# Layer-norm's beta added to three output tiles by an accumulating SBUF-to-SBUF transfer that GpSimd issues, in place of three GpSimd additions

## The chip, the cores and the metric

One core of one Trainium2 chip. The metric is the device time of one execution in microseconds (us). Engines go by the profile's names: PE is TensorE (PEld its weight loads), DVE is VectorE, ACT is ScalarE, POOL is GpSimd, SP is SyncE, which here only issues transfers.

## The reference

Cross-attention of 16 batches of 512 rows with a context of 120 rows each, a residual, and a layer norm:

```python
B, T, E, M, L = 16, 512, 512, 120, 256
q = emb @ Wq + bq                     # (B, T, E)
k = latent @ Wk + bk                  # (B, M, E)
v = latent @ Wv + bv
w = softmax(q @ k.T / sqrt(E), axis=1)      # over the 512 rows
x = w @ v + emb
mu, var = mean(x, -1), var(x, -1)
out = (x - mu) * rsqrt(var + 1e-6) * gamma + beta
```

Everything is float32, and gamma and beta are drawn, not ones and zeros.

## The kernel before

One batch is 128 partitions by four tiles j = 0 to 3 of 512 elements (`RJ` = 4). The program is software-pipelined in slots: in slot s, PE turns x of batch s and computes its scores, and multiplies probabilities and values of batch s-1; DVE adds the residual of batch s-1 and takes part of its statistics; ACT, POOL and DVE apply the norm to batch s-2. Slots 2 to 13 come from a loop over four slots, the others (0, 1, 14 to 17) are written out. Every engine has its own program, in the order of the code, and they meet at semaphores.

The norm of a batch, one slot after its statistics:

- ACT, `normalise` (lines 619 to 625): for tiles 0 to 2 (`POOL_J` = 3) it writes x*rstd + shift into `obuf[:, k % 2]`, one of two output buffers of four tiles each. It waits for POOL's `shift` and for `obuf_free`, the landing of the store that emptied this buffer.
- POOL, `times_gamma` (line 963) and `plus_beta` (line 970): three multiplications by gamma and three additions of beta, in place.
- DVE, `center` (line 825) and `rescale` (line 832): the same for tile 3 in two instructions. `center` stands in the middle of the softmax of batch s-1: after its `softmax_bias` (795 to 800) and ahead of `softmax_scale` (805, 807), for whose result ACT's `probs_to_high` (611), DVE's `probs_to_low` (811) and PE's `product` (426) wait. It, too, waits for `obuf_free` (line 824).
- POOL then finishes the statistics of batch s-1: mean of squares (982), var + eps (986, 989), `rstd` (996), `shift` (1001). DVE's part of them ends with line 899. ACT's `normalise` of the next slot waits for `shift`.
- SP (lines 307 to 326) in slot s: the context of batch s+2 (289), x of batch s+1 (285) once that ring place is free, then the store of batch s-3 (325), which waits for `pool_out` and `dve_out`. SP waits in order: what is behind a store waits with it.

So POOL's slot is: `v_part` low half (956), gamma three times, beta three times, statistics, `rstd`, `shift`. The buffer that slot s fills is used again in slot s+2. In slots 16 and 17 POOL has one tile and DVE three; slot 17 uses the buffer of slot 15, whose store is the last one that SP issues whole.

The lines that set the store and its buffer's next use:

```python
sp.wait_ge(pool_out, POOL_J * (s - 2) - moved(s - 1))          # 323
sp.wait_ge(dve_out, s - 2)
sp.dma_start(out[...], obuf[:, (k + 1) % 2]).then_inc(obuf_free[(k + 1) % 2], 16)
act.wait_ge(obuf_free[k % 2], obuf_fills(k, r))                # 622, and DVE at 824
```

Of the kernel before, what the change touches and what calls it, by code (L numbers as in the profile page):

```python
# [37 lines left out]
P = 128  # L38
# [27 lines left out]
def cross_attention(nc, x, ctx_in, Wq, bq, Wk, bk, Wv, bv, gamma, beta, out):  # L66
# [11 lines left out]
    with ExitStack() as stack:  # L78
# [19 lines left out]
        bk_all = sb("bk_all", [P, E])  # L98
        bv_all = sb("bv_all", [P, E])
        gamma_all = sb("gamma_all", [P, E])  # L100
        beta_all = sb("beta_all", [P, E])
        junk = sb("junk", [P, EC + LC + 1, E])
        act_junk = sb("act_junk", [P, B * L + LC * E], F16)
        act_warm = sb("act_warm", [P, RJ])
# [125 lines left out]
        shift_done = sem("shift_done")  # L230
        norm_done = sem("norm_done")
        pool_gamma = sem("pool_gamma")
        pool_out = sem("pool_out")
        dve_gamma = sem("dve_gamma")
        dve_out = sem("dve_out")
        tail_out = [[sem(f"tail_out{b}_{j}") for j in range(RJ)] for b in range(TAIL)]
# [45 lines left out]
        @block.sync  # L282
        def _(sp):
            def load_x(b, k):
                sp.dma_start(xbuf[:, k], x[bass.ds(b, 1)].rearrange("o (p j) e -> p (o j) e", j=RJ))\
                    .then_inc(x_in[k], 16)

            def load_ctx(b, k):
                sp.dma_start(ctx_nat[:, k, 0:L], ctx_in[bass.ds(b, 1)].rearrange("o m l -> m (o l)"))\
                    .then_inc(ctx_loaded[k], 16)  # L290

            sp.dma_start(wk_nat[:], Wk.rearrange("(c p) f -> p c f", p=P)).then_inc(wk_in, 16)
            for h in range(2):
                f = slice(h * E // 2, (h + 1) * E // 2)
                sp.dma_start(wq_nat[:, :, f], Wq.rearrange("(c p) f -> p c f", p=P)[:, :, f]).then_inc(wq_in[h], 16)
            load_ctx(0, 0)
            all_v = ctx_all.rearrange("m (b l) -> m b l", l=L)
            for h in range(2):
                sp.dma_start(all_v[:, h * B // 2:(h + 1) * B // 2],
                             ctx_in[h * B // 2:(h + 1) * B // 2].rearrange("b m l -> m b l"))\  # L300
                    .then_inc(ctx_all_in[h], 16)
            load_x(0, 0)
            sp.dma_start(wv[:], Wv.rearrange("(c p) e -> p c e", p=P)).then_inc(wv_in, 16)
            load_ctx(1, 1)
            sp.dma_start(bv_all[:], bv.partition_broadcast(P)).then_inc(bv_in, 16)

            def slot(s, k, r):

                if is_in(s, 2, B - 2):
                    sp.wait_ge(ctx_turned, s - 1)  # L310
                    sp.wait_ge(key_done, s - 1)
                if is_in(s, 0, B - 2):
                    load_ctx(s + 2, (k + 2) % RING)
                if is_in(s, 3, B - 1):
                    sp.wait_ge(norm_done, POOL_J * (s - 2))
                    sp.wait_ge(dve_gamma, (RJ - POOL_J) * (s - 2))
                if is_in(s, 0, B - 1):
                    load_x(s + 1, (k + 1) % RING)
                if is_slot(s, 0):
                    sp.dma_start(gamma_all[:], gamma.partition_broadcast(P)).then_inc(norm_in, 16)  # L320
                    sp.dma_start(beta_all[:], beta.partition_broadcast(P)).then_inc(norm_in, 16)
                if is_in(s, 3, B + 3 - TAIL):
                    sp.wait_ge(pool_out, POOL_J * (s - 2) - moved(s - 1))
                    sp.wait_ge(dve_out, s - 2)
                    sp.dma_start(out[bass.ds(s - 3, 1)].rearrange("o (p j) e -> p (o j) e", j=RJ),
                                 obuf[:, (k + 1) % 2]).then_inc(obuf_free[(k + 1) % 2], 16)

            slots(sp, slot, loop_from=3, end=B + 3 - TAIL)

            for b in range(B - TAIL, B):  # L330
                share = pool_share(b + 2)
                for j in (*range(share, RJ), *range(share)):
                    sp.wait_ge(tail_out[b - B + TAIL][j], 1)
                    sp.dma_start(out[b].rearrange("(p j) e -> p j e", j=RJ)[:, j], obuf[:, b % 2, j])\
                        .then_inc(tail_stored, 16)
            for q in range(2):
                sp.wait_ge(obuf_free[q], 16 * ((B - TAIL) // 2 + 1))
            sp.wait_ge(tail_stored, 16 * TAIL * RJ)
# [332 lines left out]
        def _(dve):  # L671
# [115 lines left out]
            def slot(s, k, r):  # L787
# [40 lines left out]
                def rescale(j):  # L828

                    dve.wait_ge(rstd_done, s - 1)  # L830
                    dve.wait_ge(dve_gamma, (RJ - POOL_J) * (s - 2) + moved(s) + j - groups[0] + 1)
                    done = dve.scalar_tensor_tensor(obuf[:, k % 2, j, :], obuf[:, k % 2, j, :],  # L832
                                                    rstd[:, k % 2, j:j + 1], beta_all[:], ALU.mult, ALU.add)
                    if is_slot(s, B) or is_slot(s, B + 1):
                        done.then_inc(tail_out[s - B][j], 1)
                    elif j == RJ - 1:
                        done.then_inc(dve_out, 1)
# [29 lines left out]
                if is_slot(s, 1):  # L867
                    ctx_to_low(2, 2)
                    copy_v(1, 1)
                    dve.wait_ge(norm_in, 2 * 16)  # L870
                if is_in(s, 2, B - 1):
                    copy_v(s + 1, k + 1)
                if is_in(s, 1, B):
# [57 lines left out]
        def _(pool):  # L931
# [14 lines left out]
            for q in range(2):  # L946
                pool.sem_inc(obuf_free[q], 16)
            pool.wait_ge(constants_set, 3)
            pool.wait_ge(norm_in, 2 * 16)

            def slot(s, k, r):
                share = pool_share(s)
                if is_in(s, 0, B):

                    pool.wait_ge(v_high, s + 1)
                    pool.tensor_tensor(v_part[:, k % 2, LOW], v_scaled[:, k % 2], v_part[:, k % 2, HIGH],  # L956
                                       ALU.subtract).then_inc(v_low, 1)

                def times_gamma():

                    for j in range(share):
                        pool.wait_ge(norm_done, POOL_J * (s - 2) - moved(s) + j + 1)
                        pool.tensor_tensor(obuf[:, k % 2, j, :], obuf[:, k % 2, j, :], gamma_all[:], ALU.mult)\  # L963
                            .then_inc(pool_gamma, 1)

                def plus_beta():

                    for j in range(share):
                        pool.wait_ge(pool_gamma, POOL_J * (s - 2) - moved(s) + j + 1)
                        done = pool.tensor_tensor(obuf[:, k % 2, j, :], obuf[:, k % 2, j, :], beta_all[:], ALU.add)  # L970
                        done.then_inc(pool_out if is_in(s, 2, B) else tail_out[s - B][0], 1)

                if is_in(s, 2, B + 2):
                    times_gamma()
                if is_in(s, 2, B) or is_slot(s, B + 1):
                    plus_beta()
                if is_in(s, 1, B + 1):

                    squares = SQUARE_J if is_in(s, 1, B - 1) else RJ
                    pool.wait_ge(squares_done,  # L980
                                 SQUARE_J * s if squares < RJ else SQUARE_J * (B - 2) + RJ * (s - B + 2))
                    pool.tensor_tensor(square_mean[:, 0:squares], square_sum[:, 0:squares],  # L982
                                       one_over_e[:, 0:squares], ALU.mult).then_inc(square_mean_done, 1)
                    if squares < RJ:
                        pool.wait_ge(aggr_done, (RJ - SQUARE_J) * s)
                        pool.tensor_tensor(var_eps[:, squares:], mean_var[:, squares:, 1], eps_all[:, squares:],  # L986
                                           ALU.add)
                    pool.wait_ge(square_mean_done, s)
                    pool.tensor_tensor(var_eps[:, 0:squares], square_mean[:, 0:squares], eps_all[:, 0:squares],  # L989
                                       ALU.add).then_inc(var_ready, 1)  # L990
                    if is_slot(s, B):
                        pool.wait_ge(dve_out, s - 2)
                    elif is_in(s, 2, B):
                        pool.wait_ge(dve_out, s - 1)
                    pool.wait_ge(var_ready, s)
                    pool.tensor_tensor(rstd[:, (k + 1) % 2], var_eps[:], minus_half[:], ALU.pow)\  # L996
                        .then_inc(rstd_done, 1)
                    if squares < RJ:
                        pool.wait_ge(mean_negated, s)
                    pool.wait_ge(rstd_done, s)  # L1000
                    pool.tensor_tensor(shift[:], neg_mean[:, (k + 1) % 2, 0:POOL_J], rstd[:, (k + 1) % 2, 0:POOL_J],  # L1001
                                       ALU.mult).then_inc(shift_done, 1)
                if is_slot(s, B):
                    plus_beta()

# [23 lines left out]
```

## Time and profile before

| | |
|---|---|
| median of 3 runs | 229.74 us (229.37 to 231.14) |
| the profiled execution | 232.62 us, span 230.8 us |
| busy share of the span | PE 86%, DVE 81%, POOL 75%, ACT 70% |
| granted TensorE clock, mean | 0.941 of full speed |
| instructions of POOL | 192 |

The span runs from the first to the last instruction; what the profiled execution has beyond it lies outside. Times in rows are from the span's start. A timeline row gives start, duration, engine, line, operation, output and inputs, shapes and count; in brackets stands the idle time ahead of it and what ended it. Neighbouring rows overlap a little, since an instruction is read in while the one before it is written.

### The profile page before, as it was taken

The numbers are of one execution on the slowest core, as the hardware profiler recorded it, in microseconds if no ns is written. First come the engines' busy times: TensorE is split into PE (matmuls) and PEld (weight loads), VectorE is DVE, ScalarE is ACT, GpSimd is POOL, SyncE is SP. The second block draws the span as 40 slices with busy tenths as digits, with TensorE's granted clock in tenths as the row PEclk, the third lists the DMA queues.
The fourth block names the chain that finished last, engine by engine and source line by source line (L and its number), as shares of the span: only waits on it lengthen the run. The fifth ranks groups of instructions, "written<-read, shape, count | busy, mean of one in ns | idle before, by whom it ended". The sixth has DMA issues, their size and how long they took to land.

```text
span 230.8 us, 4222 instructions
## 1 busy us (share of the span) xinstructions
PE 197.4 (86%) x1168; PEld 120.6 (52%) x1168; DVE 187.6 (81%) x452; ACT 161.5 (70%) x343; POOL 173.4 (75%) x192
## 2 busy tenths in 40 slices
PE   4699599999999998999799989898999898999000
PEld 4546467657566565656455555555555555545000
DVE  0472845688989898979999898999898989869993
ACT  2426465589887888787887878787969696877610
POOL 1000100428999999999999999999999999999792
PEclk9769769999999999999999999999999999999855
DMA  6999976001364737364545555555455454040454
GB/s 152 295 209 293 351 263 227 0 4 23 159 217 172 227 162 226 159 216 170 203 182 203 182 203 182 203 182 203 182 203 182 182 183 182 3 182 1 182 191 173
DMA packets 11914, 41.04 MB, mean 178 GB/s; under 512 B 1022, under 2 KB 5886, under 8 KB 8062
## 3 DMA queue, kind: packets, MB, share of 16 engines
q1 hardware_dynamic: 11614, 40.37, 50.4%
q10 hardware_dynamic: 288, 0.52, 1.3%
q8 instruction: 5, 0.08, 0.2%
q14 instruction: 7, 0.06, 0.1%
HBM read 24.12 MB, written 16.78 MB: 177 GB/s over the span
## 4 chain that ended last, share of the span: by engine, by line
POOL 56%; issue 16%; DMA 9%; PE 7%; DVE 5%; DVEq 1%; ACT 1%; SPq 1%; POOLq 1%
POOL obuf L963 20%; POOL obuf L970 18%; DMA obuf<-in_ctx 8%; POOL rstd L996 6%; POOL v_part L956 6%; POOL square_mean L982 3%; PE g_ps L404 2%; PE s_ps L434 2%; DMA out<-obuf 2%; POOL var_eps L986 1%; POOL var_eps L989 1%; DVE obuf L832 1%; DVEq L78 1%; PE v_ps L393 1%; PE xT_ps L412 1%
## 5 line engine op out<-in xcount | busy, mean ns | idle before, releaser
L963 POOL TENSOR_TENSOR obuf<-obuf,gamma_all 128x512 f32<-128x512 f32 x44 | 61.0, 1411 | 1.6 <-ACT obuf L624 1.6
L970 POOL TENSOR_TENSOR obuf<-obuf,beta_all 128x512 f32<-128x512 f32 x44 | 57.9, 1344 | 0.1
L434 PE MATMUL s_ps<-xT,gT 128*120 128x512 f32 x120 | 54.7, 598 | 0.0
L426 PE MATMUL pv_ps<-v_part,prob_part 120*128 120x512 f16 x135 | 36.1, 381 | 7.6 <-DVE xbuf L843 3.0
L624 ACT ACTIVATE obuf<-xbuf,shift,rstd 128x512 f32<-128x512 f32 x44 | 32.8, 805 | 11.3 <-POOL shift L1001 11.3
L561 ACT ACTIVATE xT<-xT_ps 128x512 f32<-128x512 f32 x64 | 34.3, 588 | 5.1 <-PE xT_ps L412 5.1
L412 PEld LDWEIGHTS xT_ps<-ident,xbuf 128*128 128x128 f32 x256 | 30.4, 143 | 11.4 <-issue 8.6
L434 PEld LDWEIGHTS s_ps<-xT,gT 128*120 128x120 f32 x120 | 22.2, 186 | 24.8 <-issue 16.2
L412 PE MATMUL xT_ps<-ident,xbuf 128*128 128x128 f32 x256 | 34.2, 278 | 1.1 <-DMA xbuf<-in_x 0.9
L843 DVE SCALAR_TENSOR_TENSOR xbuf<-pv_ps,back_y,xbuf 128x512 f32<-128x512 f32 x45 | 32.4, 741 | 0.1
L956 POOL TENSOR_TENSOR v_part<-v_scaled,v_part 120x512 f16<-120x512 f32 x16 | 19.6, 1222 | 14.8 <-ACT v_part L594 14.3
L567 ACT ACTIVATE gT<-g_ps,u_col,back_g 128x120 f32<-128x120 f32 x64 | 23.6, 457 | 6.2 <-PE g_ps L404 6.2
L832 DVE SCALAR_TENSOR_TENSOR obuf<-obuf,rstd,beta_all 128x512 f32<-128x512 f32 x20 | 27.5, 1392 | 0.0
L615 ACT ACTIVATE square_junk<-xbuf,neg_mean 128x512 f32<-128x512 f32 x36 | 25.7, 716 | 0.9 <-POOL square_mean L982 0.6
L404 PE MATMUL g_ps<-ctxT,qk_part 128*128 128x120 f16 x384 | 23.9, 222 | 1.9 <-DVE qk_part L738 1.8
L404 PEld LDWEIGHTS g_ps<-ctxT,qk_part 128*128 128x128 f16 x384 | 22.5, 101 | 3.1 <-ACT qk_part L573 2.0
L426 PEld LDWEIGHTS pv_ps<-v_part,prob_part 120*128 120x128 f16 x135 | 10.4, 97 | 24.9 <-DVE prob_part L811 7.1
L393 PE MATMUL v_ps<-wv_part,ctxT 128*120 128x512 f16 x96 | 23.4, 379 | 0.0
L856 DVE BATCH_NORM_STATS2 stats<-xbuf 128x6 f32<-128x512 f32 x28 | 19.3, 689 | 0.5
L996 POOL TENSOR_TENSOR rstd<-var_eps,minus_half 128x4 f32<-128x4 f32 x16 | 16.6, 1040 | 2.2
L605 ACT ACTIVATE s_ps<-s_ps,s_bias 120x512 f32<-120x512 f32 x15 | 9.9, 663 | 11.5 <-DVE s_bias L800 11.4
L742 DVE SCALAR_TENSOR_TENSOR ctxT<-ctx_ps,scale,ctxT 128x240 f16<-128x240 f32 x16 | 7.5, 468 | 11.3 <-ACT ctxT L557 11.3
(122 smaller groups left out, 278.0 us busy)
## 6 DMA issues: line engine op xcount, KB each, us to landing
xbuf<-in_x SPq DMA_DIRECT2D x16, 1024.0 KB, 4.8
out<-obuf SPq DMA_DIRECT2D x14, 1024.0 KB, 4.2
out<-obuf SPq DMA_DIRECT2D x8, 256.0 KB, 2.5
ctx_nat<-in_ctx SPq DMA_DIRECT2D x16, 120.0 KB, 4.3
obuf<-in_ctx SPq DMA_DIRECT2D x2, 960.0 KB, 15.5
wq_nat<-in_L_xattn_Wq SPq DMA_DIRECT2D x2, 512.0 KB, 8.9
wk_nat<-in_L_xattn_Wk SPq DMA_DIRECT2D x1, 512.0 KB, 5.8
wv<-in_L_xattn_Wv SPq DMA_DIRECT2D x1, 512.0 KB, 13.9
```

What stands on the lines that cost most here:

```text
L404: mm = pe.matmul(g_v[:, e, :], qk_part[:, of_w, c, e * P:(e + 1) * P], ctxT[:, k % 2, of_ctx, c, :], start=(n == 0), stop=(n == len(steps) ...
L412: mm = pe.transpose(xT_ps[e % 2][:, j, :], xbuf[:, k, j, e * P:(e + 1) * P], ident[:])
L426: mm = pe.matmul(banks[j], prob_part[:, of_p, j * P:(j + 1) * P], v_part[:, k % 2, of_v, :], start=(n == 0), stop=(n == len(PASSES) - 1))
L434: mm = pe.matmul(s_bank(s)[0:M, :], gT[:, k % 2, e, :], xT[:, e, :], start=(e == 0), stop=(e == EC - 1))
L561: act.activation(xT[:, e, :].rearrange("p (j q) -> p j q", q=P), xT_ps[e % 2][:], ACT.Copy)\
L624: act.activation(obuf[:, k % 2, j, :], xbuf[:, kn, j, :], ACT.Identity, bias=shift[:, j:j + 1], scale=rstd[:, k % 2, j:j + 1]).then_inc(no ...
L832: done = dve.scalar_tensor_tensor(obuf[:, k % 2, j, :], obuf[:, k % 2, j, :], rstd[:, k % 2, j:j + 1], beta_all[:], ALU.mult, ALU.add)
L843: dve.scalar_tensor_tensor(xbuf[:, kb, j, :], (last_y_ps if is_slot(s, B) else y_ps)[j], back_y[:], xbuf[:, kb, j, :], ALU.mult, ALU.add, ...
L956: pool.tensor_tensor(v_part[:, k % 2, LOW], v_scaled[:, k % 2], v_part[:, k % 2, HIGH], ALU.subtract).then_inc(v_low, 1)
L963: pool.tensor_tensor(obuf[:, k % 2, j, :], obuf[:, k % 2, j, :], gamma_all[:], ALU.mult)\
L970: done = pool.tensor_tensor(obuf[:, k % 2, j, :], obuf[:, k % 2, j, :], beta_all[:], ALU.add)
L996: pool.tensor_tensor(rstd[:, (k + 1) % 2], var_eps[:], minus_half[:], ALU.pow)\
```

## The change

`beta_all` becomes three copies of beta side by side (three loads in place of one), so that one transfer can cover tiles 0 to 2. In slots 2 to 15 POOL no longer adds beta; at the end of its slot, behind `shift`, it issues one transfer with `accum_op=add` from `beta_all` to `obuf[:, k % 2, 0:3]` (128 partitions by 1536 float32, 768 KB). SP's store waits for that transfer's semaphore (`beta_added`, one for each buffer) in place of `pool_out`. Slots 16 and 17 keep their one addition on POOL.

```diff
-        beta_all = sb("beta_all", [P, E])
+        beta_all = sb("beta_all", [P, POOL_J, E])
...
-        pool_out = sem("pool_out")
+        beta_added = [sem(f"beta_added{q}") for q in range(2)]
...
-                    sp.dma_start(beta_all[:], beta.partition_broadcast(P)).then_inc(norm_in, 16)
+                    for j in range(POOL_J):
+                        sp.dma_start(beta_all[:, j], beta.partition_broadcast(P)).then_inc(norm_in, 16)
...
-                    sp.wait_ge(pool_out, POOL_J * (s - 2) - moved(s - 1))
+                    sp.wait_ge(beta_added[(k + 1) % 2], obuf_fills(k - 1, r))
...
+                def add_beta():
+
+                    pool.dma_start(obuf[:, k % 2, 0:POOL_J, :], beta_all[:], accum_op=ALU.add)\
+                        .then_inc(beta_added[k % 2], 16)
+
                 def plus_beta():
 
-                    for j in range(share):
-                        pool.wait_ge(pool_gamma, POOL_J * (s - 2) - moved(s) + j + 1)
-                        done = pool.tensor_tensor(obuf[:, k % 2, j, :], obuf[:, k % 2, j, :], beta_all[:], ALU.add)
-                        done.then_inc(pool_out if is_in(s, 2, B) else tail_out[s - B][0], 1)
+                    pool.wait_ge(pool_gamma, POOL_J * (s - 2) - moved(s) + 1)
+                    pool.tensor_tensor(obuf[:, k % 2, 0, :], obuf[:, k % 2, 0, :], beta_all[:, 0], ALU.add)\
+                        .then_inc(tail_out[s - B][0], 1)
...
-                if is_in(s, 2, B) or is_slot(s, B + 1):
+                if is_slot(s, B + 1):
                     plus_beta()
...
+                    if is_in(s, 2, B):
+                        pool.wait_ge(pool_gamma, POOL_J * (s - 1))
                     pool.wait_ge(rstd_done, s)
                     pool.tensor_tensor(shift[:], neg_mean[:, (k + 1) % 2, 0:POOL_J], rstd[:, (k + 1) % 2, 0:POOL_J],
                                        ALU.mult).then_inc(shift_done, 1)
+                if is_in(s, 2, B):
+                    add_beta()
```

POOL, one slot of the loop before, from the last multiplication by gamma to the first instruction of the next slot:

```order
L962 REGISTER_ALU
L963 TENSOR_TENSOR obuf<-obuf,gamma_all 128x512 [waits norm_done]
L970 TENSOR_TENSOR obuf<-obuf,beta_all 128x512 [waits pool_gamma] x3
L980 REGISTER_ALU
L982 TENSOR_TENSOR square_mean<-square_sum,one_over_e 128x2 [waits squares_done]
L986 TENSOR_TENSOR var_eps<-mean_var,eps_all 128x2 [waits aggr_done]
L989 TENSOR_TENSOR var_eps<-square_mean,eps_all 128x2 [waits square_mean_done]
L996 TENSOR_TENSOR rstd<-var_eps,minus_half 128x4 [waits var_ready,dve_out]
L1001 TENSOR_TENSOR shift<-neg_mean,rstd 128x3 [waits rstd_done,mean_negated]
L955 REGISTER_ALU
L956 TENSOR_TENSOR v_part<-v_scaled,v_part 120x512 [waits v_high]
```

The same place on POOL in the change (its lines stand a few numbers lower in the file):

```order
L963 REGISTER_ALU
L964 TENSOR_TENSOR obuf<-obuf,gamma_all 128x512 [waits norm_done]
L985 REGISTER_ALU
L987 TENSOR_TENSOR square_mean<-square_sum,one_over_e 128x2 [waits squares_done]
L991 TENSOR_TENSOR var_eps<-mean_var,eps_all 128x2 [waits aggr_done]
L994 TENSOR_TENSOR var_eps<-square_mean,eps_all 128x2 [waits square_mean_done]
L1001 TENSOR_TENSOR rstd<-var_eps,minus_half 128x4 [waits var_ready,dve_out]
L1006 REGISTER_ALU [waits mean_negated]
L1008 TENSOR_TENSOR shift<-neg_mean,rstd 128x3 [waits rstd_done,pool_gamma]
L969 DMA obuf<-beta_all 128x1536
L956 REGISTER_ALU
L957 TENSOR_TENSOR v_part<-v_scaled,v_part 120x512 [waits v_high]
```

The three additions are gone from between gamma and the statistics, and one DMA stands behind `shift`, ahead of the next slot's `v_part`.

SP, one slot of the loop before, where a store stands between the loads of x and of the context:

```order
L285 ISA [waits dve_gamma,norm_done]
L285 DMA xbuf<-in_x 128x2048
L325 ISA [waits dve_out,pool_out]
L325 DMA out<-obuf 128x2048
L289 ISA [waits key_done,ctx_turned]
L289 DMA ctx_nat<-in_ctx 120x256
```

The same place on SP in the change:

```order
L285 ISA [waits dve_gamma,norm_done]
L285 DMA xbuf<-in_x 128x2048
L324 ISA
L326 ISA [waits dve_out,beta_added1]
L326 DMA out<-obuf 128x2048
L289 ISA [waits key_done,ctx_turned]
L289 DMA ctx_nat<-in_ctx 120x256
```

The order on SP is the same but for one instruction that sets the count to wait for (L324); the store waits for the accumulating transfer's landing where it waited for POOL's third addition, and the next context and x wait behind it.

## Rows read from the trace of the kernel before

**Rows 1.** The page: where the chain of work that ended last goes, by engine and line.

```profile
POOL 56%; issue 16%; DMA 9%; PE 7%; DVE 5%; DVEq 1%; ACT 1%; SPq 1%; POOLq 1%
```

**Rows 2.** POOL's timeline, one slot in the steady state.

```profile
112.01 0.19 POOL L1001 TENSOR_TENSOR shift<-neg_mean,rstd 128x3 f32<-128x3 f32 x1
...
113.28 4.19 POOL L963 TENSOR_TENSOR obuf<-obuf,gamma_all 128x512 f32<-128x512 f32 x3
117.42 3.93 POOL L970 TENSOR_TENSOR obuf<-obuf,beta_all 128x512 f32<-128x512 f32 x3
...
122.42 1.02 POOL L996 TENSOR_TENSOR rstd<-var_eps,minus_half 128x4 f32<-128x4 f32 x1
123.58 0.19 POOL L1001 TENSOR_TENSOR shift<-neg_mean,rstd 128x3 f32<-128x3 f32 x1
```

**Rows 3.** POOL's timeline: `shift` of slots 2 and 13, the ends of eleven slots.

```profile
65.22 0.19 POOL L1001 TENSOR_TENSOR shift<-neg_mean,rstd 128x3 f32<-128x3 f32 x1
...
193.50 0.19 POOL L1001 TENSOR_TENSOR shift<-neg_mean,rstd 128x3 f32<-128x3 f32 x1
```

**Rows 4.** PE's timeline: the first instructions of two slots' scores, slots 1 to 3.

```profile
46.94 3.60 PE L434 MATMUL s_ps<-xT,gT 128*120 128x512 f32 x8
...
57.47 3.60 PE L434 MATMUL s_ps<-xT,gT 128*120 128x512 f32 x8
...
68.46 1.88 PE L434 MATMUL s_ps<-xT,gT 128*120 128x512 f32 x4
```

**Rows 5.** The load of beta (DMA issues, SP's timeline) and POOL's first wait for it.

```profile
beta_all<-in_L_xattn_beta SPq DMA_DIRECT2D x1, 256.0 KB, 16.3
...
16.39 0.62 SPq L321 DMA_DIRECT2D beta_all<-in_L_xattn_beta  x1
...
42.48 1.16 POOL L956 TENSOR_TENSOR v_part<-v_scaled,v_part 120x512 f16<-120x512 f32 x1 [14.10 <-ACT v_part L594]
```

**Rows 6.** The page: DMA issues, KB each, median us from issue to landing.

```profile
xbuf<-in_x SPq DMA_DIRECT2D x16, 1024.0 KB, 4.8
out<-obuf SPq DMA_DIRECT2D x14, 1024.0 KB, 4.2
out<-obuf SPq DMA_DIRECT2D x8, 256.0 KB, 2.5
```

**Rows 7.** SP's timeline around one store.

```profile
114.62 0.33 SPq L285 DMA_DIRECT2D xbuf<-in_x  x1
121.51 0.35 SPq L325 DMA_DIRECT2D out<-obuf  x1
```

**Rows 8.** DVE and PE: who uses the stored buffer and the loaded x next.

```profile
132.80 0.75 DVE L825 SCALAR_TENSOR_TENSOR obuf<-xbuf,mean_var,gamma_all 128x512 f32<-128x512 f32 x1
...
130.26 1.04 PE L412 MATMUL xT_ps<-ident,xbuf 128*128 128x128 f32 x8
```

**Rows 9.** DVE's and POOL's timelines, slot 2 and the end of slot 1.

```profile
50.48 0.17 DVE L899 BATCH_NORM_AGGREGATE mean_var<-stats 128x2 f32<-128x6 f32 x1
...
52.15 0.75 DVE L825 SCALAR_TENSOR_TENSOR obuf<-xbuf,mean_var,gamma_all 128x512 f32<-128x512 f32 x1
...
60.95 0.17 DVE L899 BATCH_NORM_AGGREGATE mean_var<-stats 128x2 f32<-128x6 f32 x1
...
52.46 0.49 POOL L1001 TENSOR_TENSOR shift<-neg_mean,rstd 128x3 f32<-128x3 f32 x1
```

**Rows 10.** The DMA view of 100 to 136 us, GB/s in 40 slices.

```profile
GB/s 428 300 146 0 164 355 419 228 0 0 0 82 419 373 291 137 0 73 319 428 346 0 0 0 137 419 319 298 130 0 118 300 428 319 0 0 0 146 437 291
```

**Rows 11.** DVE, ACT and POOL from slot 15 to the end.

```profile
201.57 1.64 DVE L825 SCALAR_TENSOR_TENSOR obuf<-xbuf,mean_var,gamma_all 128x512 f32<-128x512 f32 x1
...
220.16 2.06 DVE L825 SCALAR_TENSOR_TENSOR obuf<-xbuf,neg_mean,gamma_all 128x512 f32<-128x512 f32 x3
...
213.49 0.19 ACT L615 ACTIVATION_READ_ACCUMULATOR square_junk<-xbuf,neg_mean 128x1 f32 x1
...
215.73 0.23 POOL L1001 TENSOR_TENSOR shift<-neg_mean,rstd 128x3 f32<-128x3 f32 x1
```

More of the change, by code:

```diff
@@ L832, in rescale @@
                     done = dve.scalar_tensor_tensor(obuf[:, k % 2, j, :], obuf[:, k % 2, j, :],
-                                                    rstd[:, k % 2, j:j + 1], beta_all[:], ALU.mult, ALU.add)
+                                                    rstd[:, k % 2, j:j + 1], beta_all[:, 0], ALU.mult, ALU.add)
                     if is_slot(s, B) or is_slot(s, B + 1):
@@ L869, in slot @@
                     copy_v(1, 1)
-                    dve.wait_ge(norm_in, 2 * 16)
+                    dve.wait_ge(norm_in, (1 + POOL_J) * 16)
                 if is_in(s, 2, B - 1):
@@ L948, in _ @@
             pool.wait_ge(constants_set, 3)
-            pool.wait_ge(norm_in, 2 * 16)
+            pool.wait_ge(norm_in, (1 + POOL_J) * 16)
             def slot(s, k, r):
```

## The prediction

> **What bounds the kernel now.** Read first the chain of waits [rows 1]: 56% of the span runs over POOL, far more than over any other engine, although PE and DVE have the larger busy shares on the page. Then POOL's timeline [rows 2]: from one `shift` to the next it has no gap of size; `v_part`, 4.19 us of gamma, 3.93 us of beta, statistics, `rstd`, `shift`. The eleven slots from `shift` of slot 2 to that of slot 13 take 193.50 - 65.22 = 128.28 us, 11.66 each [rows 3]. The limit behind it shows where POOL is still idle ahead of its work, in slots 1 and 2: PE's scores start at 46.94 and 57.47, 10.53 us apart, and once POOL is full already 10.99 [rows 4]. So 10.53 us is what PE, with DVE and ACT beside it, needs for a slot, and at most 1.13 us a slot can be gained.
>
> **What the change removes.** 3.93 us from each POOL slot. POOL then needs 11.57 - 3.93 = 7.64 us plus the issue of one transfer [rows 2]; unless that issue takes over 2.9 us, POOL no longer bounds. The added wait on `pool_gamma` ahead of `shift` is for work that is long over: nothing. The two more loads of beta come behind all that the head waits for: beta was issued at 16.39 and landed 16.3 us later, at 32.7; POOL's first wait that includes it ended at 42.48, and for ACT [rows 5]. 512 KB more take at most another 2 x 2.5 us [rows 6], and 37.7 is still early: nothing.
>
> **What it moves.** The store. It waited for the third addition, which ended ahead of the statistics; the store was issued 0.16 us after that, at 121.51 (117.42 + 3.93 = 121.35) [rows 2, 7]. Now it waits for `shift`, then for the issue and landing of the accumulating transfer. Call x the time from the end of `shift` until that has landed. The store lands 4.2 us after its issue [rows 6] and frees the buffer that DVE's `center` (L825) and ACT's `normalise` write two slots on. Before, the store of 121.51 had landed at 125.7 and its buffer's next `center` ran at 132.80 [rows 8]: 7 us of cover. After, the path closes into a loop over two slots, whose sum I take:
>
> - `center` to the end of DVE's statistics: 52.15 to 60.95 + 0.17, that is 8.97 us, in slot 2, where POOL held nothing up [rows 9]. `softmax_scale`, `probs_to_low`, `rescale` and the residuals are queued behind `center` on DVE, and PE's products wait for `probs_to_low`: a late `center` shifts all of it.
> - from there to the end of `shift` on a POOL that is ready: 50.48 + 0.17 to 52.46 + 0.19 (`shift` as in the steady slot), 2.0 us [rows 2, 9].
> - x, then 0.16 to the store's issue, 4.2 to its landing, and 0.1 (an estimate, by the 0.16 above) for DVE to see it.
>
> Together 15.43 + x us for two slots. That equals PE's 2 x 10.53 at x = 5.6 and today's 2 x 11.66 at x = 7.9.
>
> **x, which no row shows.** The transfer has 768 KB. Stores take 2.5 us for 256 KB and 4.2 for 1024 KB [rows 6], so 1.7 us for each 768 KB more: a plain copy of this size would land after 2.5 + 512/768 x 1.7 = 3.63 us. To add, the engines must read the destination as well as beta: another 768 KB of reads, 1.7 us, if it only costs its bytes. From below x is 3.63 (the reads overlap, and POOL's issue costs no more than SP's). From above, the destination's read and the sum are two transfers in a row, 7.3, and POOL's issue takes as long as its slowest small instruction, `rstd` with 1.02 [rows 2]: 8.3 us. I take 3.63 + 1.7 and 0.8 for an issue made by POOL, nearer to `rstd` than to `shift`'s 0.19: x = 6.1. Other transfers add little: the store, and x of a later batch behind it, take 4.9 us of a slot at the highest rate of 428 GB/s, with slices at 0 between [rows 10], and they now start when the accumulation has landed.
>
> The Trainium skill, "DMA: Bandwidth & Descriptors", section on the anatomy of a transfer issued by GpSimd, gives 2.0 us plus bytes over 436 GB/s, 3.8 us for 786,432 bytes; "Collectives: The Full Stack", on the bandwidth ceiling, says that an add inside the DMA engines is limited by its two source reads, at half a copy's rate. Both together make 5.6, an estimate; the trace's 4.2 us for 1024 KB agrees with the first within 0.3, and no row here shows the second. With 5.6 the sum below would give 221.8 in place of 225.3.
>
> What waits on SP behind the store: the next context and x. The x load of 114.62 (landing 4.8 us later [rows 6, 7]) is used by PE at 130.26 [rows 8], over 10 us on. It now goes out behind the store of the `shift` that ends at 112.20 [rows 2]: 112.2 + 6.1 + 0.2, and 1.2 for two issues ahead of it (each 0.35 and a gap), 119.7. Behind the store's data it needs 4.2 + 1.7 + 1 us at most and lands at 126.6: still covered, and POOL's issue hides in POOL's spare 2.9 us.
>
> **The sum**, on the profiled execution (232.62 us, span 230.8):
>
> - `shift` of slot 2 no longer waits for beta: 60.95 + 0.17 + 2.0 = 63.1 in place of 65.4 [rows 3, 9]; slot 3 follows PE, 63.1 + 10.53 = 73.65.
> - Slots 3 to 13 are five turns of the loop, 5 x (15.43 + 6.1) = 107.7: `shift` of slot 13 ends at 181.3, not 193.69. Gain 12.4 us.
> - The tail gives much of it back. `center` of slot 15 comes 6.1 + 4.46 = 10.56 us after that, at 191.9. From there to slot 15's `shift` was 201.57 to 215.96, 14.4 us [rows 11]; beta beside it had stretched `center` to 1.64 us from 0.75 [rows 9, 11] (0.9 goes), and `shift` comes 2.3 us after ACT's last square (213.68), which with POOL free is 2.0: 13.2. So 205.1, and the last whole store lands for `center` of slot 17 another 10.56 later, at 215.7. That was 220.16 [rows 11], and from there to the end 10.64 us, which stay: 226.3.
>
> 230.8 - 226.3 = 4.5 us less: 228.1 for the profiled execution, and 225.3 from the median of 229.74. The time goes with x by 7 us for each us (five turns, and twice in the tail): at x = 6.74 the change gains nothing. A measurement of this kernel tells about 1%, 2.3 us: faster means x under 6.4, slower x over 7.06.
>
> **Rivals.**
>
> 1. PE is the floor: x is 5.6 or less, the loop no longer decides, and slots run at 10.53. The time is 225.3 - 7 x 0.5 = 221.8, and then only the tail's two waits count: at x = 3.63, 2 x 2 us less, 217.9. For it: bytes that only overlap. Against: a second read of 768 KB that no row lets vanish.
> 2. The issue is held up by DVE. By the sums above `shift` ends close to the next slot's `center` (which comes 10.56 us after the `shift` of the slot before, and half a turn is 10.77). That POOL and DVE hold each other up shows in `center`, 1.64 beside beta against 0.75 [rows 9, 11]. If POOL's issue waits for one `center`, 0.75 us, x is 6.85 and the time 230.5: no change. The Trainium skill, "SBUF — State Buffer", section "SBUF: two separate sides", says that GpSimd cannot write a transfer's descriptors while DVE holds the port that both share; by that rule this rival holds, and no row shows a transfer issued by POOL.
> 3. Slower: the accumulation lands too late. Place: the wait for `obuf_free` ahead of `center`, L825. If the add runs as two transfers in a row, x is 8.3, a slot takes (15.43 + 8.3) / 2 = 11.87, over today's 11.66, and the last whole store comes 2 x 2.2 us later again: 225.3 + 7 x 2.2 = 240.7. It decides from x = 7.06. For it: two dependent steps in each element, and a landing that the store now has to wait for; against: the engines that run at 428 GB/s may do both reads in one stream.
>
> That the change does not relieve POOL (an issue of 3.9 us, as long as the additions) is part of the third: x would be over 8.
>
> **How the numbers follow.** Forecast (x from 5.6 to 6.4): 0.32. Rival 1: 0.20. Rival 2, with all x from 6.4 to 7.06: 0.16. Rival 3: 0.32. So faster by over 1%: 0.52; within 1%: 0.16; slower: 0.32. The forecast's own range is 221.8 to 227.4. The whole range goes from 218 (x = 3.63) to 241 (x = 8.3), and leaves out an x above both bounds.
>
> **What would show it.** Right: POOL with gaps ahead of gamma, `shift` to `shift` under 11.2 us, DVE's `center` waiting for the store's landing, some 10.6 us after `shift`, and again in slot 17; the issue-to-landing time of the new transfer near 6. Wrong: `center` that never waits and PE without gaps (rival 1), POOL's issue beside a long DVE instruction (rival 2), waits at `center` of more than 2 us in each slot (rival 3).

## The result: 11.5% slower, and the profile after

| | before | after |
|---|---|---|
| median, us | 230.38 (229.37 to 231.14, 4 runs) | 259.52 (256.23 to 261.55, 4 runs) |
| ratio | | 1.1154, 95% interval 1.1051 to 1.1256 |
| profiled execution, us | 232.62, span 230.8 | 256.23, span 254.4 |

Two of the four runs after the change took 261.5 us at a lower granted clock, and the ratio is over the other two, 256.23 and 257.54 us. The forecast was 225.3 us, faster; its range ended at 241. In the changed kernel gamma is line 964, `shift` 1008, the issue of the transfer 969, `center` 826, `rescale` 833, the residual 844, the store 326.

The page of the changed kernel: busy shares and chain (these answer to [rows 1]), the group of `rescale`, and the transfers:

```profile
PE 196.5 (77%) x1168; PEld 121.1 (48%) x1168; DVE 207.3 (81%) x452; ACT 161.4 (63%) x343; POOL 126.4 (50%) x164
...
PE 30%; issue 21%; DVE 21%; ACT 11%; DMA 11%; DVEq 2%; SPq 1%; POOL 1%; ACTq 0%; POOLq 0%
...
L833 DVE SCALAR_TENSOR_TENSOR obuf<-obuf,rstd,beta_all 128x512 f32<-128x512 f32 x20 | 51.0, 2567 | 0.0
...
xbuf<-in_x SPq DMA_DIRECT2D x16, 1024.0 KB, 6.4
out<-obuf SPq DMA_DIRECT2D x14, 1024.0 KB, 4.7
obuf<-beta_all POOLq DMA_DIRECT2D x14, 768.0 KB, 5.8
```

The same group before the change:

```profile
L832 DVE SCALAR_TENSOR_TENSOR obuf<-obuf,rstd,beta_all 128x512 f32<-128x512 f32 x20 | 27.5, 1392 | 0.0
```

POOL was relieved as meant: 50% busy in place of 75%, 1% of the chain in place of 56%. The transfer lands 5.8 us after its issue, close to the forecast's estimate. But DVE's `rescale`, which the change doesn't touch, costs 23.5 us more. Who pays is in PE's waits, after and before (us in total, times, longest):

```profile
PE pv_ps L427 <- DVE xbuf L844: 26.8, 9, 3.3
```

```profile
PE pv_ps L426 <- DVE xbuf L843: 3.0, 11, 0.5
```

PE's product needs the buffer that DVE's residual (844) empties, and the residual is queued behind `rescale`. 26.8 - 3.0 = 23.8 us, and the span grew by 254.4 - 230.8 = 23.6. That these two agree so closely is chance, because other terms cancel. From `center` of slot 3 to `center` of slot 15 the changed kernel takes 220.89 - 59.25 = 161.6 us for twelve slots (before: 138.8). At the 10.51 us a slot that e3 below shows they would take 126.1. Of the 35.5 us between, PE's nine waits of 3 us behind a long `rescale` are 26.8, and some 8 are PE's work at a lower clock in three slots (last section). So the loop loses about 35 us in its long slots; that first eats the 12.6 us that relieving POOL was worth, and the rest shows as loss. Outside these slots the head is 3.6 us shorter and the tail 4.3 longer. One of the nine slots, DVE and POOL, beside one of the five slots in which `rescale` is short (118.64):

```profile
114.91 1.48 POOL L957 TENSOR_TENSOR v_part<-v_scaled,v_part 120x512 f16<-120x512 f32 x1
114.98 1.97 DVE L826 SCALAR_TENSOR_TENSOR obuf<-xbuf,mean_var,gamma_all 128x512 f32<-128x512 f32 x1
118.64 0.74 DVE L833 SCALAR_TENSOR_TENSOR obuf<-obuf,rstd,beta_all 128x512 f32<-128x512 f32 x1
118.72 4.26 POOL L964 TENSOR_TENSOR obuf<-obuf,gamma_all 128x512 f32<-128x512 f32 x3 [2.32 <-ACT obuf L625]
126.42 0.75 DVE L826 SCALAR_TENSOR_TENSOR obuf<-xbuf,mean_var,gamma_all 128x512 f32<-128x512 f32 x1
126.85 0.37 POOL L1008 TENSOR_TENSOR shift<-neg_mean,rstd 128x3 f32<-128x3 f32 x1
127.29 0.94 POOL L969 DMA_DIRECT2D obuf<-beta_all  x1
127.95 1.49 POOL L957 TENSOR_TENSOR v_part<-v_scaled,v_part 120x512 f16<-120x512 f32 x1
129.04 4.62 DVE L833 SCALAR_TENSOR_TENSOR obuf<-obuf,rstd,beta_all 128x512 f32<-128x512 f32 x1
129.12 3.98 POOL L964 TENSOR_TENSOR obuf<-obuf,gamma_all 128x512 f32<-128x512 f32 x3
133.28 0.36 SPq L326 DMA_DIRECT2D out<-obuf  x1
133.58 0.74 DVE L844 SCALAR_TENSOR_TENSOR xbuf<-pv_ps,back_y,xbuf 128x512 f32<-128x512 f32 x1
138.35 0.17 DVE L900 BATCH_NORM_AGGREGATE mean_var<-stats 128x2 f32<-128x6 f32 x1
```

`rescale` asks at 129.04, while `v_part` runs, and ends at 133.66; `v_part` ends at 129.44 and the third gamma at 133.10, so `rescale` ended 0.56 us behind all of them. The nine long slots and the five short ones differ in one more row: in each short one POOL's first gamma waits for ACT (2.32 us at 118.72, 0.69 to 2.81 in the five), in none of the long ones does it wait. Before the change `rescale` asked beside `v_part` too:

```profile
112.16 1.16 POOL L956 TENSOR_TENSOR v_part<-v_scaled,v_part 120x512 f16<-120x512 f32 x1
112.31 1.56 DVE L832 SCALAR_TENSOR_TENSOR obuf<-obuf,rstd,beta_all 128x512 f32<-128x512 f32 x1
113.28 4.19 POOL L963 TENSOR_TENSOR obuf<-obuf,gamma_all 128x512 f32<-128x512 f32 x3
```

There it ended at 113.87, 0.55 us behind `v_part`'s end (113.32), and the first gamma waited for it. The Trainium skill, "SBUF — State Buffer", section "Who interferes with whom", says that a DVE instruction with two inputs in SBUF and a GpSimd instruction that reads SBUF exclude each other, the first holding the ports for its whole length. The row of before agrees (one instruction waited out, 1.56 us); the row of after shows more than that sentence tells: four instructions in a row waited out.

One coincidence hides the cause in this slot: the third gamma (133.10) and the landing of the transfer (127.29 + 5.8 = 133.09, with SP's store at 133.28) end together, so the row alone does not tell which of them `rescale` waited for.

The tail, which answers to [rows 11], did what the forecast said:

```profile
234.82 0.94 POOL L969 DMA_DIRECT2D obuf<-beta_all  x1
...
244.60 3.08 DVE L826 SCALAR_TENSOR_TENSOR obuf<-xbuf,neg_mean,gamma_all 128x512 f32<-128x512 f32 x3 [5.55 <-DMA out<-obuf]
```

### The profile page after: what moved, and what is told of

It is laid out like the page before. It is cut to its first block, busy times and chain, and to the rows that moved or that the text cites. A ratio compares the mean times of both kernels' runs of the same rounds, so it can differ in the third digit from the quotient of the medians.

```text
span 254.4 us, 4215 instructions
## 1 busy us (share of the span) xinstructions
PE 196.5 (77%) x1168; PEld 121.1 (48%) x1168; DVE 207.3 (81%) x452; ACT 161.4 (63%) x343; POOL 126.4 (50%) x164
## 4 chain that ended last, share of the span: by engine, by line
PE 30%; issue 21%; DVE 21%; ACT 11%; DMA 11%; DVEq 2%; SPq 1%; POOL 1%; ACTq 0%; POOLq 0%
PE s_ps L435 16%; DMA obuf<-in_ctx 7%; DVE xbuf L844 5%; PE pv_ps L427 5%; DVE obuf L833 4%; PE xT_ps L413 3%; ACT xT L562 2%; DMA obuf<-beta_all 2%; DVE obuf L826 2%; PE v_ps L394 2%; DVE s_max L796 2%; PE g_ps L405 2%; ACT s_ps L606 2%; ACT prob_part L612 2%; ACT obuf L625 2%
## 5 line engine op out<-in xcount | busy, mean ns | idle before, releaser
L964 POOL TENSOR_TENSOR obuf<-obuf,gamma_all 128x512 f32<-128x512 f32 x44 | 59.1, 1454 | 13.6 <-ACT obuf L625 13.6
L435 PE MATMUL s_ps<-xT,gT 128*120 128x512 f32 x120 | 59.8, 645 | 0.0
L427 PE MATMUL pv_ps<-v_part,prob_part 120*128 120x512 f16 x135 | 35.2, 385 | 27.2 <-DVE xbuf L844 26.8
L833 DVE SCALAR_TENSOR_TENSOR obuf<-obuf,rstd,beta_all 128x512 f32<-128x512 f32 x20 | 51.0, 2567 | 0.0
L435 PEld LDWEIGHTS s_ps<-xT,gT 128*120 128x120 f32 x120 | 23.9, 200 | 28.4 <-issue 24.1
L987 POOL TENSOR_TENSOR square_mean<-square_sum,one_over_e 128x2 f32<-128x2 f32 (+1 forms) x16 | 3.6, 223 | 55.3 <-ACT square_junk L616 55.3
L427 PEld LDWEIGHTS pv_ps<-v_part,prob_part 120*128 120x128 f16 x135 | 11.6, 98 | 40.5 <-DVE xbuf L844 29.4
L957 POOL TENSOR_TENSOR v_part<-v_scaled,v_part 120x512 f16<-120x512 f32 x16 | 22.7, 1418 | 11.5 <-ACT v_part L595 11.5
L405 PE MATMUL g_ps<-ctxT,qk_part 128*128 128x120 f16 x384 | 22.8, 216 | 1.8 <-DVE qk_part L739 1.8
L796 DVE TENSOR_REDUCE s_max<-s_ps 120x1 f32<-120x512 f32 x15 | 10.3, 688 | 7.1 <-PE s_ps L435 6.8
L612 ACT ACTIVATE prob_part<-s_ps,s_by 120x512 f16<-120x512 f32 x15 | 10.3, 688 | 7.6 <-DVE s_by L808 7.5
```

The lines of the kernel that those rows point to most:

```text
L405: mm = pe.matmul(g_v[:, e, :], qk_part[:, of_w, c, e * P:(e + 1) * P], ctxT[:, k % 2, of_ctx, c, :], start=(n == 0), stop=(n == len(steps) ...
L427: mm = pe.matmul(banks[j], prob_part[:, of_p, j * P:(j + 1) * P], v_part[:, k % 2, of_v, :], start=(n == 0), stop=(n == len(PASSES) - 1))
L435: mm = pe.matmul(s_bank(s)[0:M, :], gT[:, k % 2, e, :], xT[:, e, :], start=(e == 0), stop=(e == EC - 1))
```

## The experiments

Twelve kernels, e1 to e12; each ratio is to the kernel before, run beside it. Three theories for the long `rescale` stood at the start. P: the order at the port that DVE and POOL share; displaced by the issue, `v_part` and the gammas get ahead of `rescale`. D: the transfer's own reads and writes in SBUF hold `rescale` up. L, the forecast's third rival: the landing is too late.

**e1, the issue moved right behind the gammas** (a product of two columns on scratch carries the wait for them).

```diff
                     times_gamma()
+                if is_in(s, 2, B):
+                    pool.wait_ge(pool_gamma, POOL_J * (s - 1))
+                    pool.tensor_tensor(spare[:, 0:2], eps_all[:, 0:2], minus_half[:, 0:2], ALU.mult)
+                    add_beta()
...
-                if is_in(s, 2, B):
-                    add_beta()
```

> The transfer is issued right behind the three multiplications by gamma (a 0.2 us POOL instruction on scratch carries the wait for them) instead of behind shift. Theory P (port order): the 0.94 us issue behind shift pushes v_part and the gammas so late that DVE's rescale asks while they run back to back and gets its turn only after all three. With the issue out of that place rescale takes 0.74 to 1.6 us, slots 10.5 to 11 us, the last whole store no longer waits for slot 15's shift: 217 to 224 us. Theory D (the accumulation's own reads and writes in SBUF hold rescale up): rescale no longer falls into the transfer either, same numbers. Theory L (the store lands too late): also relieved, but some waits ahead of center stay if the landing is the cause.

**e2, the gammas wait for `rescale`** (`pool.wait_ge(dve_out, s - 1)` ahead of `times_gamma()` in slots 2 to 15).

> The change as it is, but in slots 2 to 15 POOL starts gamma only when DVE's rescale of the slot has ended. Theory P: rescale falls from 4.5 to at most 1.6 us (only v_part can be ahead of it), slots from 13.5 to about 10.7 to 11.2, the wait for the last whole store in slot 17 stays, 224 to 230 us. Theory D: the transfer still runs beside rescale, which stays at 4.5 us, and the time at 255 us or over. Theory L: little change, 250 us or over.

**e3, beta left out on POOL's tiles**, no transfer, the store waits for gamma. **e4, e3 with a power of 1.0 us** on scratch behind `shift`, where the issue was.

> Leaves out beta on POOL's three tiles in slots 2 to 15: no additions and no transfer, the store waits for gamma. It shows what taking 3.9 us from POOL's slot is worth alone. All theories: PE sets the slot with 10.5 us, rescale 0.74 us in most slots, 214 to 220 us.

> As the one before (beta on POOL's three tiles in slots 2 to 15 left out, no transfer), with a POOL instruction of 1.04 us on scratch at the place of the issue, behind shift. Theory P: the place alone is enough, rescale takes over 4 us in most slots, slots near 13.5 us, 240 to 250 us. Theory D and theory L: nothing is transferred, rescale 0.74 us, slots 10.5 us, as the run without the instruction within 2 us.

Measured: e1 226.01 us (ratio 0.9774, 0.9661 to 0.9887), e2 238.41 (1.0305, 1.0228 to 1.0383), e3 217.50 (0.9406, 0.9300 to 0.9511), e4 216.76 (0.9374, 0.9282 to 0.9466). In e1 `rescale` takes 0.74 us in the loop, and the transfer is the same: D, the theory of the transfer's own bytes, loses its ground. e2 says so directly, with `rescale` in the middle of the transfer's flight, and shows what else is wrong:

```profile
131.31 0.94 POOL L969 DMA_DIRECT2D obuf<-beta_all  x1 [0.25 <-issue]
131.97 1.48 POOL L957 TENSOR_TENSOR v_part<-v_scaled,v_part 120x512 f16<-120x512 f32 x1
136.59 3.74 POOL L964 TENSOR_TENSOR obuf<-obuf,gamma_all 128x512 f32<-128x512 f32 x3 [3.14 <-DVE obuf L833]
131.47 2.53 DVE L826 SCALAR_TENSOR_TENSOR obuf<-xbuf,mean_var,gamma_all 128x512 f32<-128x512 f32 x1 [1.02 <-DMA out<-obuf]
135.69 0.74 DVE L833 SCALAR_TENSOR_TENSOR obuf<-obuf,rstd,beta_all 128x512 f32<-128x512 f32 x1
```

`rescale` takes 0.74, but `center`, asking 0.16 us after the issue began, waits out the issue and `v_part` (until 133.45) and takes 2.53. e4 contradicts P as it was put: a microsecond's displacement alone leaves `rescale` at 0.74 to 0.92. e3 is the floor: `center` to `center` is 10.51 us over six slots (101.55 to 164.60), the 10.53 of [rows 4].

**e5 and e6: is it only the displacement?** As e4, with about 1.5 and 2.0 us of work behind `shift`.

```diff
+                if is_in(s, 2, B):
+                    pool.tensor_tensor(spare[:, 0], eps_all[:], minus_half[:], ALU.pow)
+                    pool.tensor_tensor(spare[:, 1], eps_all[:], minus_half[:], ALU.mult)   # e5: three such; e6: one more pow
```

> Beta is left out on GpSimd's three tiles and nothing is transferred; behind `shift` GpSimd does one power of 1.0 us and three small products (about 0.2 us each) on scratch, so that `v_part` begins some 0.6 us later than in e4, at the place it has after the change. Theory Q (GpSimd's queue: where the first of the three gammas is already free to go when `v_part` ends, GpSimd goes over without a gap and VectorE's `rescale`, asking while `v_part` runs, waits for all three): `rescale` 4 to 4.6 us in most slots of the loop, time 235 to 252 us. Theory W (it is the transfer, by its issue or by its bytes, that sets `rescale` behind the gammas): `rescale` 0.74 to 1.5, time 216 to 220.

> As e5, with two powers of 1.0 us behind `shift`, so that `v_part` is asked about when `rescale` is. Theory Q: a tie; where `v_part` comes first, `rescale` 4 us or more and 240 to 255 us; where `rescale` comes first it takes 0.74 and only `v_part` and the product that needs it are late, by about 0.7 us per slot: 222 to 228 us. Theory W: `rescale` 0.74 to 1.5 in all slots.

**e8: the issue without the bytes** (the changed kernel with a transfer of 2 KB on scratch; beta is left out on POOL's tiles).

```diff
-                    pool.dma_start(obuf[:, k % 2, 0:POOL_J, :], beta_all[:], accum_op=ALU.add)\
+                    pool.dma_start(spare[:, k % 2, :], beta_all[:, 0, 0:RJ], accum_op=ALU.add)\
```

> The changed kernel with the transfer shrunk to four numbers of each partition, in scratch (2 KB in place of 768 KB; beta is left out on GpSimd's tiles, the waits stay). Theory Q: `v_part` begins where it did, so `rescale` stays at 4 to 4.6 us in most slots; the store goes out 3 to 4 us sooner and the tail's late store goes: 238 to 250 us. Theory W by the bytes in flight: `rescale` 0.74 to 1.5 and 216 to 222 us. Theory W by the issue: 4 us or more, as Q (e5 and e7 tell these two apart).

Measured: e5 218.41 us (ratio 0.9468, 0.9415 to 0.9522), e6 218.89 (0.9489, 0.9432 to 0.9546), e8 252.36 and 258.18 us; its rows are from the run of 258.18, and the other is 9% above the kernel before too. In e6 most `rescale` take 1.6 to 1.7 us, none more. e5:

```profile
126.52 1.17 POOL L958 TENSOR_TENSOR v_part<-v_scaled,v_part 120x512 f16<-120x512 f32 x1
127.03 1.20 DVE L834 SCALAR_TENSOR_TENSOR obuf<-obuf,rstd,beta_all 128x512 f32<-128x512 f32 x1
127.64 2.96 POOL L965 TENSOR_TENSOR obuf<-obuf,gamma_all 128x512 f32<-128x512 f32 x2
```

e8:

```profile
129.15 0.94 POOL L973 DMA_DIRECT2D spare<-beta_all  x1
129.81 1.48 POOL L961 TENSOR_TENSOR v_part<-v_scaled,v_part 120x512 f16<-120x512 f32 x1
131.02 4.50 DVE L835 SCALAR_TENSOR_TENSOR obuf<-obuf,rstd,beta_all 128x512 f32<-128x512 f32 x1
131.09 3.86 POOL L968 TENSOR_TENSOR obuf<-obuf,gamma_all 128x512 f32<-128x512 f32 x3
```

Theory Q (a gamma that is ready when `v_part` ends is enough) falls: in e5 `rescale` asks in the middle of `v_part`, gamma stands right behind, and `rescale` still gets its turn at `v_part`'s end (127.69 + 0.54 = 128.23). In e8, without the bytes (the 2 KB land 2.1 us after their issue) but with the issue, it is 4.50. So the issue does it, and the landing at 133.09 was a coincidence (L falls for the long `rescale`). The rows also differ in how POOL's instructions follow each other: in e5 gamma's record begins 0.05 us before `v_part`'s ends (126.52 + 1.17 - 127.64), in e8 0.20 us, in the changed kernel 0.32 (127.95 + 1.49 - 129.12). The overlap starts with the issue: in the changed kernel `v_part` begins 0.28 us before the issue's own end and its record is 1.49 us long in place of 1.16. That made theory R: behind an issue POOL's instructions form an unbroken row, which ends only where one of them waits, and `rescale` gets its turn behind the whole row.

**e7, the issue behind `v_part`** (the next slot's `v_part` moved to the end of the slot, ahead of the issue).

> The changed kernel whole, with GpSimd's order shift, v_part of the next slot, issue of the transfer, gammas (the issue was ahead of `v_part`). Theory Q: `rescale` asks while the issue (0.94 us) runs, which doesn't hold it up, and gets in ahead of the gammas: 0.74 to 1.3 us; the transfer lands 1.2 us later (x about 7.0), loop 15.43+7.0 = 22.4 over two slots, 11.2 us per slot, and the last whole store late as before: 229 to 235 us. Theory W: `rescale` stays at 4 us or more, 248 to 262 us.

Measured: 236.60 us (ratio 1.0261, 1.0215 to 1.0308); `rescale` 0.74 in the loop, and `center` waits for a store in 13 slots, 19.8 us in all. R allows this: in most slots the first gamma, which now follows the issue, waits 1.4 to 3.2 us for ACT, so the row is broken. In two slots nothing waits (62.20 and 144.49); there `rescale` asks in the last 0.2 to 0.3 us of the issue, 0.08 us ahead of gamma, and gets its turn at once. So an issue does not hold up everything that asks while it runs.

**e9 and e10: break the row.** e9 adds a wait behind `v_part`, e10 a 4-column product and a wait ahead of it. The transfer and its place stay.

```diff
+                if is_in(s, 2, B):                       # e9
+                    pool.wait_ge(v_low, s + 1)
                 if is_in(s, 2, B + 2):
                     times_gamma()
...
                     add_beta()
+                    pool.tensor_tensor(spare[:, 0], eps_all[:], minus_half[:], ALU.mult).then_inc(spare_set, 1)   # e10
+                    pool.wait_ge(spare_set, s - 1)
```

> The changed kernel whole, with one wait more: GpSimd waits for the end of its own `v_part` before it takes up the three gammas. Nothing moves and no data is late by more than about 0.1 us. Theory R (row: behind the issue GpSimd takes up each next instruction some 0.3 us before the one ahead ends, until a wait breaks the row; the first gamma is then in line when `v_part` ends, and VectorE's `rescale` gets its turn only behind the third): with the row broken `rescale` waits for `v_part` alone and takes 1.1 to 1.5 us, the loop over two slots that the forecast was made of sets the pace, and the last whole store stays late: 225 to 236 us. Theory S (the issue itself, whatever follows it, sets VectorE behind GpSimd's work until that has run dry): `rescale` stays at 4 us or more in most slots, 248 to 262 us.

> The changed kernel whole, with the row broken one place sooner: behind the issue GpSimd does a product of 4 columns (about 0.2 us) on scratch and waits for its end before `v_part`, nothing stands between `v_part` and the gammas. Theory R: behind the break the gamma is taken up only at `v_part`'s end, as without a transfer (e5), so `rescale` takes 1.1 to 1.7 us; `v_part` comes about 0.5 us later: 226 to 238 us. If the state that the issue leaves outlasts a wait: `rescale` 4 us or more in most slots, 248 to 262 us.

**e11 and e12: slot 15's beta on POOL again**, so that the last whole store waits for no transfer; e11 on e9, e12 on e10.

> e9, and in the last slot of whole stores (15) GpSimd adds beta itself behind its gammas, as before the change, so that this store doesn't wait for a transfer. Theory R and the forecast's tail: `center` of slot 17 no longer waits 5 us for a store, 4 to 6 us less than e9: 220 to 231 us. If the tail's wait is covered by something else: within 2 us of e9.

> The changed kernel with both repairs: the break ahead of `v_part` (e10) and slot 15's beta added by GpSimd itself (e11). By theory R and the forecast's loop and tail: `rescale` 0.74 to 1.5 us, `center` still waits 0.2 to 2 us for the store of two slots before in most slots of the loop (as in e10), and the 5.5 us at slot 17 go: 4 to 6 us less than e10, 227 to 230 us, so that of the change nothing is gained or lost beyond 1.5 %. If the waits in the loop come from the late tail or from the row: 222 us or less.

Measured: e9 239.30 us (1.0404, 1.0340 to 1.0469), e10 233.19 (1.0139, 1.0057 to 1.0220), e11 233.86 (1.0144, 1.0083 to 1.0205), e12 228.59 (0.9882, 0.9832 to 0.9932). e9, two slots:

```profile
119.43 0.94 POOL L969 DMA_DIRECT2D obuf<-beta_all  x1 [0.25 <-issue]
120.01 2.12 DVE L826 SCALAR_TENSOR_TENSOR obuf<-xbuf,mean_var,gamma_all 128x512 f32<-128x512 f32 x1 [1.44 <-DMA out<-obuf]
120.09 1.48 POOL L957 TENSOR_TENSOR v_part<-v_scaled,v_part 120x512 f16<-120x512 f32 x1
...
133.11 1.48 POOL L957 TENSOR_TENSOR v_part<-v_scaled,v_part 120x512 f16<-120x512 f32 x1
134.21 0.94 DVE L833 SCALAR_TENSOR_TENSOR obuf<-obuf,rstd,beta_all 128x512 f32<-128x512 f32 x1
134.75 4.01 POOL L964 TENSOR_TENSOR obuf<-obuf,gamma_all 128x512 f32<-128x512 f32 x3 [0.16 <-POOL v_part L957]
```

e10, a slot, then `center` of the next two and, between them, the end of DVE's statistics:

```profile
96.58 0.94 POOL L971 DMA_DIRECT2D obuf<-beta_all  x1 [0.24 <-issue]
97.23 0.53 POOL L1014 TENSOR_TENSOR spare<-eps_all,minus_half 128x4 f32<-128x4 f32 x1
98.26 1.16 POOL L959 TENSOR_TENSOR v_part<-v_scaled,v_part 120x512 f16<-120x512 f32 x1 [0.50 <-POOL spare L1014]
98.59 1.38 DVE L835 SCALAR_TENSOR_TENSOR obuf<-obuf,rstd,beta_all 128x512 f32<-128x512 f32 x1
99.38 4.19 POOL L966 TENSOR_TENSOR obuf<-obuf,gamma_all 128x512 f32<-128x512 f32 x3
107.69 0.75 DVE L828 SCALAR_TENSOR_TENSOR obuf<-xbuf,mean_var,gamma_all 128x512 f32<-128x512 f32 x1 [1.28 <-DMA out<-obuf]
116.32 0.17 DVE L902 BATCH_NORM_AGGREGATE mean_var<-stats 128x2 f32<-128x6 f32 x1
119.88 0.75 DVE L828 SCALAR_TENSOR_TENSOR obuf<-xbuf,mean_var,gamma_all 128x512 f32<-128x512 f32 x1 [1.97 <-DMA out<-obuf]
```

A wait of 0.16 us in POOL's program turns 4.6 us of `rescale` into 0.94 (e9; it asks 1.10 us behind the start of `v_part`, in the changed kernel 1.09), and so does a break ahead of `v_part` (e10: the record of `v_part` is 1.16 us long again, gamma follows at 0.04 us, `rescale` takes 1.38). R holds in both. In e9 the row that is left, issue and `v_part`, still catches a `center` that the store has made late (2.12 us); e10 breaks that one too and is 6 us better. Both are slower than the kernel before, because `center` now waits for the store, in the loop and in slot 17: the forecast's loop and tail. The tail is priced twice: e9 to e11 2.6%, e10 to e12 2.6%, 6 us. With both repairs (e12) the change is 1.2% faster than the kernel before.

Six times lie above the nearest range that stood ahead of the run: e1 by 2.0 us, e2 8.4, e7 1.6, e8 2.4, e9 3.3, e11 2.9. In all of these but e8 `center` waits for a store in several slots of the loop, which the ranges had too small or left out.

## Why the prediction was wrong, step by step

The parts, each as a ratio to the kernel before: beta off POOL -5.9% (e3); the wait for the landing in the loop +4.8% (e3 to e12, the break's own half microsecond a slot included); the tail +2.6% (e12 to e10); the row behind the issue +10.1% (e10 to the changed kernel). They add up to 11.5% because each is the step from one kernel to the next; each is known to about 1%. The split holds for this order of repairs only: in the changed kernel itself no `center` but slot 17's waits for a store, because its slots of 13.5 us leave the store time. There the row alone makes the loop slower than e3's, by the 35 us above, near the 34 us (4.8 + 10.1 = 14.9%) that the two terms give.

- *What bounds before, and what beta on POOL is worth:* right. Without it slots run at 10.51 us (e3); forecast 10.53.
- *"`center` to the end of DVE's statistics ... 8.97 us, in slot 2, where POOL held nothing up":* this step failed. Its row had a `rescale` of 0.74 us, and the sum took it for the loop, where POOL stands beside it. The page had a warning, though not of this size: `rescale` at 1392 ns on average, 1.56 beside `v_part`. With the issue it became 4.5 to 4.9 us in nine slots, 3 us of it on PE's path. The term then measures 138.35 + 0.17 - 126.42 = 12.10 us; with the row broken, in e10, it is 116.32 + 0.17 - 107.69 = 8.80, so the 8.97 was right for a DVE that POOL leaves alone. The forecast weighed the wrong pair as well: rival 2 let POOL's issue wait for DVE's `center`; the runs show DVE waiting for POOL. The issue takes 0.93 to 0.95 us in 13 of its 14 places (1.17 in the first), and 0.93 in e7 beside a `center` (131.46), so rival 2 is not seen; what `center` did hold up was `shift` ahead of the issue, 0.7 us in place of 0.19 in two slots.
- *x = 6.1:* right for the transfer alone, and too small at the forecast's own pace. In the changed kernel, with slots of 13.5 us, the landing came 133.09 - 127.22 = 5.9 us after `shift`. From the issue on the row reads 5.8, and e8's 2 KB read 2.1, so the 768 KB themselves take 3.7 us. The prediction's estimate by the Trainium skill ("DMA: Bandwidth & Descriptors", section "Anatomy of one DMA", with the rate halved for the add's two source reads by "Collectives: The Full Stack", section "The bandwidth ceiling") was 5.6, and the trace's 5.8 agrees with it within 0.2. But in e10, with the row gone, `shift` ends at 130.72 and the store goes out at 138.41, x + 0.16 = 7.7. There the x load, issued at 128.04 behind the store, is still under way when the transfer starts; the forecast said "Other transfers add little". (Its highest rate was misread as well: [rows 10] has a slice of 437 GB/s, not 428, which changes its 4.9 us by 0.1.) In e1, from 99 us on, transfer and x load start within 0.6 to 1.4 us of each other, and both take about twice as long:

```profile
xbuf<-in_x SPq DMA_DIRECT2D x16, 1024.0 KB, 10.1
out<-obuf SPq DMA_DIRECT2D x14, 1024.0 KB, 4.4
obuf<-beta_all POOLq DMA_DIRECT2D x14, 768.0 KB, 10.4
```

- *The loop of 15.43 + x over two slots:* right in form. With x = 7.5, e10's mean over the five slots from 107.69, it gives 11.5 us a slot; e10's `center` goes from 107.69 to 165.41 in these five, 11.5 each. So without the row the forecast would still have come out on the wrong side, by rival 3's place (L825, past x = 7.06), with x from a busy queue and not from two transfers in a row: 1.4% slower in e10.
- *The tail:* right. `center` of slot 17 waits 5.55 us for the last whole store, in the changed kernel as in e2 and e10; e11 and e12 take that away and gain 6 us.

## What to carry to other kernels

A duration taken from a slot where the neighbour engine is idle is a lower bound; before it enters a sum, look at the same instruction's mean and longest on the page. When a GpSimd queue issues a transfer, look at which of its instructions stand behind the issue without a wait and which VectorE instruction with two SBUF inputs falls there; move the issue to a place where GpSimd waits next (e1, 2.3% faster than before, interval 1.1 to 3.4%), or put a wait there. A transfer that replaces engine work also becomes a link that stores wait for: add the loads that start in the same stretch to its landing time.

## What the runs showed of the hardware

- Behind an issue (0.94 us on POOL) the records of POOL's instructions overlap by 0.2 to 0.3 us in place of 0.05, until one of them waits, and a VectorE instruction with two inputs in SBUF waits for the whole row: `rescale` took 4.5 us behind `v_part` and three gammas, `center` 2.53 us behind issue and `v_part`; each takes 0.74 alone. Two breaks (e9, e10) show that it is the unbroken row, and e8 that 2 KB do it as well as 768. Why an issue has this effect no run tells.
- The long slots don't all keep the clock. Stretches of the changed kernel (busy us by engine, then the granted clock, DMA share, GB/s):

```profile
102.50:118.60 16.10, 13.09 (x74) 7.36 (x70) 14.26 (x26) 9.32 (x22) 8.06 (x11) 0.89 0.76 217
126.40:139.90 13.50, 10.32 (x68) 6.46 (x67) 13.14 (x27) 9.09 (x20) 7.84 (x11) 1.00 0.78 238
196.90:213.40 16.50, 13.71 (x73) 7.71 (x70) 13.03 (x27) 9.40 (x21) 7.92 (x11) 0.79 0.79 214
```

PE idles 2.8 to 3.3 us in each of the nine long slots, and in three of them the granted clock then fell from 2.4 to 1.2 GHz for a time: the two shown with 0.89 and 0.79, and the one from 61.95 to 78.38 with 0.90 over the slot. These three are 16.1 to 16.5 us long in place of 13.5, with 13.1 to 13.7 us of PE work in place of some 10.6. The slot behind each takes only 10.3 to 10.4 us, because there the first gamma waits for ACT and `rescale` is short, so a fall and the slot behind it together cost no more than two long slots (26.5 to 26.8 us against some 27.1). What picks those three stays open.
